# Variances with one token to a partition, inverses spread by TensorE into PSUM, and part of the pre-summing moved to DVE, in an adaLN block on Trainium2

## The reference, cut to what matters

```python
mod = (silu(c) @ wmod).reshape(2, 6, 1, -1)
sa, ca, ga, sb, cb, gb = mod[:, 0], ..., mod[:, 5]
ga, gb = (sign * max(|g|, 0.25) for g in (ga, gb))
h = layernorm(x) * (1 + ca) + sa
# per feature: a 2x2 softmax of inner products over the 2048 tokens mixes the two samples
x = x + ga * (h + msg(h))
h = layernorm(x) * (1 + cb) + sb
x = x + gb * ffn(h)       # down( silu(h Wgate) * (h Wup) ), width 2752
```

## Time and profile before

| what | value |
|---|---|
| median of 3 runs | 2818.89 us (2817.76 to 2823.97) |
| profiled execution, its own time | 2821.63 us |
| its span | 2819.8 us |
| mean granted TensorE clock, share of full | 0.992 |
| TensorE busy (matmul) | 2750.6 us, 98% |
| DVE busy | 1545.2 us, 55% |
| ACT busy | 1059.7 us, 38% |
| POOL busy | 156.1 us, 6% |

### The profile page before, as it was taken

The page is one execution under the profiler, slowest core; times in us unless marked ns, Lnnn a source line. Parts: engine busy times, 40 slices in busy tenths (PEclk is TensorE's granted clock), DMA queues, the critical chain, the costliest instruction groups (busy, mean ns, idle before and its releaser), DMA issues.

```text
span 2819.8 us, 32541 instructions
## 1 busy us (share of the span) xinstructions
PE 2750.6 (98%) x11784; PEld 2157.2 (77%) x11784; DVE 1545.2 (55%) x2057; ACT 1059.7 (38%) x1616; POOL 156.1 (6%) x206
## 2 busy tenths in 40 slices
PE   8988999998999999999999899999999999999999
PEld 3336887786888886788887788887788888888887
DVE  6988777764455534455443433335446446446544
ACT  4656455553243432334423211112343333333332
POOL 5200011000010000000100000000000000000000
PEclk9999999999999999999999999999999999999999
DMA  8675999989788879888879999999757657657654
GB/s 343 241 288 195 334 329 325 334 301 342 267 300 304 305 256 299 287 309 301 294 271 283 348 358 344 352 348 320 252 212 256 227 210 250 233 211 245 245 202 165
DMA packets 359711, 795.77 MB, mean 282 GB/s; under 512 B 25760, under 2 KB 154016, under 8 KB 350848
## 3 DMA queue, kind: packets, MB, share of 16 engines
q1 hardware_dynamic: 341648, 721.32, 73.3%
q0 software_dynamic: 17088, 59.78, 6.2%
q10 hardware_dynamic: 816, 12.58, 1.1%
HBM read 553.26 MB, written 240.32 MB: 281 GB/s over the span
## 4 chain that ended last, share of the span: by engine, by line
PE 86%; DMA 3%; issue 1%; SPq 1%; ACT 1%; DVE 1%; DVEq 0%; ACTq 0%
PE ps L1588 19%; PE ps L1589 19%; PE ps L1590 19%; PE ps L1651 10%; PE ps L1652 10%; PE ps L1653 10%; DMA x_raw_P<-xr_dram 1%; DMA h_dram<-ww 1%; DMA w_raw<-wdn 0%; SPq L397 0%; SPq L388 0%; DMA whl_dram<-w_lo_P 0%; PE ps L1598 0%; ACT x_raw_P L737 0%; PE ps L1599 0%
## 5 line engine op out<-in xcount | busy, mean ns | idle before, releaser
L1588 PE MATMUL ps<-x_hi_P,w_slot 128*128 128x512 f32 (+1 forms) x1848 | 724.5, 392 | 23.1 <-ACT vv L803 10.5
L1589 PE MATMUL ps<-x_lo_P,w_slot 128*128 128x512 f32 (+1 forms) x1848 | 723.2, 391 | 0.0
L1590 PE MATMUL ps<-x_hi_P,w_slot 128*128 128x512 f32 (+1 forms) x1848 | 722.9, 391 | 0.0
L1651 PE MATMUL ps<-hh,w_hi 128*128 128x512 f32 (+1 forms) x1232 | 481.1, 391 | 3.3 <-DVE w_lo L1354 2.0
L1652 PE MATMUL ps<-hl,w_hi 128*128 128x512 f32 (+1 forms) x1232 | 480.9, 390 | 0.0
L1653 PE MATMUL ps<-hh,w_lo 128*128 128x512 f32 (+1 forms) x1232 | 479.9, 389 | 0.0
L1588 PEld LDWEIGHTS ps<-x_hi_P,w_slot 128*128 128x128 f32 (+1 forms) x1848 | 344.4, 186 | 104.9 <-ACT vv L803 11.7
L1590 PEld LDWEIGHTS ps<-x_hi_P,w_slot 128*128 128x128 f32 (+1 forms) x1848 | 344.4, 186 | 78.3
L1589 PEld LDWEIGHTS ps<-x_lo_P,w_slot 128*128 128x128 f32 (+1 forms) x1848 | 344.5, 186 | 77.4
L1354 DVE TENSOR_TENSOR w_lo<-w_raw,w_hi 128x1408 fp32r<-128x1408 f32 x112 | 181.7, 1623 | 212.6 <-ACT w_hi L870 212.6
L1651 PEld LDWEIGHTS ps<-hh,w_hi 128*128 128x128 f32 (+1 forms) x1232 | 231.6, 188 | 53.3 <-DVE w_lo L1354 2.4
(11 more groups left out here) (181 smaller groups left out, 2651.6 us busy)
## 6 DMA issues: line engine op xcount, KB each, us to landing
w_slot<-whl_dram SPq DMA_DIRECT2D x420, 512.0 KB, 6.1
w_raw<-wds_dram SPq DMA_DIRECT2D x64, 704.0 KB, 4.6
hl_raw<-h_dram SPq DMA_DIRECT2D x56, 768.0 KB, 7.0
h_dram<-hb SPq DMA_DIRECT2D x30, 1280.0 KB, 9.8
whl_dram<-w_hi SPq DMA_DIRECT2D x140, 256.0 KB, 3.4
whl_dram<-w_lo_P SPq DMA_DIRECT2D x140, 256.0 KB, 4.2
w_raw<-wdn SPq DMA_DIRECT2D x48, 704.0 KB, 5.0
hl_raw<-h_dram SPq DMA_DIRECT2D x28, 1024.0 KB, 9.8
```

What stands on the lines that cost most here:

```text
L1588: mm(bank, hi[:, w], x_hi[name][:, k, :], start=fresh and k == 0, stop=False, skip_group_check=not fresh)
L1589: mm(bank, hi[:, w], x_lo[name][:, k, :], start=False, stop=False, skip_group_check=not fresh)
L1590: ins = mm(bank, lo[:, w], x_hi[name][:, k, :], start=False, stop=k == KH - 1, skip_group_check=not fresh)
L1651: mm(bank, hi[0:n, w], hh[stage % 2][0:n, j, :], start=fresh and j == 0, stop=False, skip_group_check=not fresh)
```

## The change

The variance is formed with tokens on the partitions: for each 128 tokens, TensorE takes 128 columns of `sq_pair` as weights and one column of ones as the moving side, so a chunk's variances are a 128x4 tile in PSUM. Root (ACT) and reciprocal (DVE) work on 128x4. ACT then makes four diagonal 128x128 matrices from the identity and these inverses (`diagonal`), and TensorE multiplies them by ones (`spread`), which puts the 512 inverses into every row of a PSUM bank; `normalise` reads that bank. For u = 1 the banks are the ones of `ps_mean[1]`, so the means of u = 1 of half 1 wait until half 0 is normalised. DVE adds tiles 0 to 3 of three of the four chunks of half 0, POOL of one. Stores of the normalised pairs are issued in halves of 2 MB. The order on TensorE is written anew.

```diff
+    eye_all = sb("eye_all", [P], F32, 184 * K)
+    std = sb("std", [2, 2, NTB], F32, 185 * K)
+    inv = sb("inv", [2, 2, NTB], F32, 185 * K + 64)
+    diag = sb("diag", [2, NTB, P], F32, 192 * K)
...
+    RSTD_BANK = (6, 2)
...
@@ POOL
                 if t == 0:
-                    sum_tiles(0, 0)
                     sum_tiles(0, 1)
-                    sum_tiles(1, 0)
-                    add_squares(0, 0)
-                    sum_tiles(1, 1)
-                else:
-                    add_squares(0, 0)
+                add_squares(0, 0)
                 add_squares(0, 1)
@@ ACT
+                def diagonal(u, h):
+                    i = t * 4 + 2 * u + h
+                    act.wait_ge(inv_ready, i + 1)
+                    if i >= 2:
+                        act.wait_ge(rstd_ready, i - 1)
+                    for b in range(NTB):
+                        ins = s.activation(diag[:, h, b, :], eye_all[:], ACT.Identity, scale=inv[:, u, h, b:b + 1])
+                    ins.then_inc(diag_ready, 1)
...
                 for u, h in ((0, 0), (0, 1), (1, 0), (1, 1)):
                     square(u, h, range(NSQ // 2))
                     if (u, h) != (0, 0):
                         root(u if h else 0, 1 - h)
                     square(u, h, range(NSQ // 2, NSQ))
+                    if (u, h) != (0, 0):
+                        diagonal(u if h else 0, 1 - h)
                 root(1, 1)
-                square_sums(0, range(KD))
-                save_xhat(0)
-                square_sums(1, range(KD // 2))
+                square_sums(0, range(KD // 2))
+                save_xhat(0, 0)
+                square_sums(0, range(KD // 2, KD - 1))
+                diagonal(1, 1)
+                square_sums(0, range(KD - 1, KD))
+                save_xhat(0, 1)
                 if t:
                     copy_rows(0)
+                square_sums(1, range(KD // 2))
+                if t == 0:
+                    save_xhat(1, 0)
+                square_sums(1, range(KD // 2, KD - 2))
+                if t:
                     copy_rows(1)
-                square_sums(1, range(KD // 2, KD))
+                square_sums(1, range(KD - 2, KD))
                 if t == 0:
-                    save_xhat(1)
+                    save_xhat(1, 1)
@@ DVE
                 def invert(u, h):
-                    v.reciprocal(rstd[:, u, h, :], std[:, h, :]).then_inc(rstd_ready, 1)
+                    v.reciprocal(inv[:, u, h, :], std[:, u, h, :]).then_inc(inv_ready, 1)
+                def sum_tiles(u, h):
...
+                    v.tensor_tensor(two, xk[:, 0:2, :], xk[:, 2:4, :], ALU.add).then_inc(presum_chain, 1)
+                    dve.wait_ge(presum_chain, summed[0])
+                    v.tensor_tensor(presums[u][:, h, :], two[:, 0, :], two[:, 1, :], ALU.add).then_inc(presum_dve, 1)
                 def normalise(u, k):
-                        v.scalar_tensor_tensor(dbuf[u][:, :, k, b, :], dbuf[u][:, :, k, b, :], 1.0,
-                                               rstd[:, u, :, b * CC:(b + 1) * CC], ALU.mult, ALU.mult,
+                        v.scalar_tensor_tensor(dbuf[u][:, :, k, b, :], ps[:, RSTD_BANK[u]:RSTD_BANK[u] + 2, b * CC:(b + 1) * CC], 1.0,
+                                               dbuf[u][:, :, k, b, :], ALU.mult, ALU.mult,
...
+                if t == 0:
+                    sum_tiles(0, 0)
                 centre(0, 0)
+                if t == 0:
+                    sum_tiles(1, 0)
                 centre(0, 1)
+                if t == 0:
+                    sum_tiles(1, 1)
                 centre(1, 0)
                 invert(0, 0)
                 centre(1, 1)
                 invert(0, 1)
...
                 for u in range(2):
-                    dve.wait_ge(rstd_ready, t * 4 + (2 * u + 4))
+                    dve.wait_ge(rstd_ready, t * 4 + (2 * u + 2))
                     for k in range(KD):
                         normalise(u, k)
...
-                        if u == 0 and k in (2, 4):
-                            invert(1, (k - 2) // 2)
+                        if u == 0 and k in (3, 5):
+                            invert(1, (k - 3) // 2)
@@ TensorE, means
-                    if t:
-                        pe.wait_ge(centred, 2 * (i + 1))
+                    if t and u == 0:
+                        pe.wait_ge(std_ready, i + 1)
+                    if t and u == 1:
+                        pe.wait_ge(xhat_ready, 4 * KD)
@@ TensorE, variances and spread
-                        mm(ps_var[h], ones[:], sq_pair[:, j % 2, :], start=j == 0, stop=j == NSQ - 1).then_inc(sq_pair_used, 1)
-                        if group is not None:
-                            modulate(group, part_of, range(2 * j, 2 * j + 2))
+                        for b in range(NTB):
+                            ins = mm(ps_mean[u][h][:, b:b + 1], sq_pair[:, j % 2, b * P:(b + 1) * P], ones[:, 0:1],
+                                     start=j == b == 0, stop=j == NSQ - 1 and b == NTB - 1)
+                        ins.then_inc(sq_pair_used, 1)
+                def spread(u, h):
+                    pe.wait_ge(diag_ready, t * 4 + (2 * u + h + 1))
+                    if t and u == 0:
+                        pe.wait_ge(xhat_ready, 2 * KD)
+                    mm(ps[:, RSTD_BANK[u] + h, :], ones[:], diag[:, h].rearrange("p b q -> p (b q)"), start=True, stop=True).then_inc(
+                        rstd_ready, 1)
@@ TensorE, order
+                means(0, 0)
+                means(0, 1)
                 if t == 0:
-                    means(0, 0)
-                    means(0, 1)
                     means(1, 0)
                     variances(0, 0)
                     means(1, 1)
                     variances(0, 1)
+                    spread(0, 0)
+                    variances(1, 0)
+                    spread(0, 1)
                     pe.wait_ge(silu_ready, 1)
-                    parts(0, range(2))
-                    variances(1, 0, 0, 2)
-                    variances(1, 1, 0, 3)
+                    parts(0, range(1))
+                    variances(1, 1)
+                    spread(1, 0)
+                    parts(0, range(1, 2))
+                    spread(1, 1)
+                    parts(0, range(2, 3))
                 else:
-                    means(0, 0)
-                    means(0, 1)
+                    parts(0, range(3, GROUP[0]))
                     means(1, 0)
                     means(1, 1)
-                    variances(0, 0, 0, 4)
-                    variances(0, 1, 0, 5)
-                    variances(1, 0, 1, 0)
-                    variances(1, 1, 1, 1)
-                    parts(1, range(2, GROUP[1]))
-            pe.wait_ge(eye_loaded, 16)
-            pe.wait_ge(centred, 16)
-            parts(2, range(4))
+                    variances(0, 0)
+                    variances(0, 1)
+                    parts(1, range(1))
+                    spread(0, 0)
+                    spread(0, 1)
+                    variances(1, 0)
+                    parts(1, range(1, 2))
+                    spread(1, 0)
+                    variances(1, 1)
+                    parts(1, range(2, 3))
+                    spread(1, 1)
+                    parts(1, range(3, GROUP[1]))
+            pe.wait_ge(eye_loaded, 32)
             turn(0, ps_mod[0], ROWS[0] + ROWS[1], 0)
             turn(1, ps_mod[0], ROWS[0] + ROWS[1], ROWS[0])
-            parts(2, range(4, GROUP[2]))
+            parts(2, range(GROUP[2]))
```

More of the change, by code:

```diff
@@ L48 @@
 PRE = (4, 0)
+NTB = T // P
 assert NPAIR == 4 and sum(GROUP) == NPART and 2 * WPART == BLOCK and GROUP[0] == GROUP[1] == 2 * WM_RING
@@ L294, in bc, with tok2 @@
         return ap[:, None, :].broadcast_to([P, n, T])
+    def tok2(ap):
+        return ap.rearrange("p h k b c -> p h k (b c)")
     def tok(ap):
@@ L552, in sum_tiles @@
                 def sum_tiles(u, h):
-                    i = 2 * u + h
-                    pool.wait_ge(x_loaded[u][h], t * 16 + 16)
-                    pool.wait_ge(mean_mm, t * 4 + (i + 1))
+                    pool.wait_ge(x_loaded[u][h], 16)
                     xk, to = tok(xbuf[u][:, h]), presums[u][:, h, :]
-                    for k in range(1, PRE[t]):
+                    for k in range(1, PRE[0]):
                         ins = g.tensor_tensor(to, xk[:, 0, :] if k == 1 else to, xk[:, k, :], ALU.add)
-                        if k < PRE[t] - 1:
+                        if k < PRE[0] - 1:
                             ins.then_inc(pool_chain, 1)
@@ L644, in _, with save_xhat @@
             for t in range(NPAIR // 2):
[L645 to L650, removed]
+                def save_xhat(u, half):
+                    act.wait_ge(xhat_ready, t * (4 * KD) + 2 * KD * u + KD * (half + 1))
+                    first, ks = 4 * t + 2 * u + 2, slice(half * KD // 2, (half + 1) * KD // 2)
+                    s.dma_start(xhat_dram[first:first + 2].rearrange("h p (k w) -> p h k w", k=KD)[:, :, ks],
+                                tok2(dbuf[u][:, :, ks])).then_inc(xh_stored[u], 16)
```

(32 more changed lines are left out.)

40 lines of the change are left out of this document (22 added, 18 removed).

## The result

The changed kernel takes 2851.79 us (median of 4 runs, 2849.61 to 2852.64) against 2821.43 (median of 4, 2817.76 to 2824.74) of the kernel before in the same comparison: 1.011 times as long, 95% interval 1.0095 to 1.0126, or 30.4 us more. The profiled execution took 2851.85 us with a span of 2850.1, 30.3 more than before. The forecast was 21.6 more, 2840.5, in the range 2826 to 2853: the result lies inside it, 1.2 us from its upper end and 11.3 from the forecast's own number.

A forecast was written before the change was run, and what follows sets the result against it. DVE was taken to set most of the first phase, TensorE's written order its last 8 us. The turn's +7.6 and +14.0 for four more parts behind it sum to +21.6 on 2818.9: 2840.5 us, range 2826 to 2853.

The forecast's parts named there:

- DVE's gain: First phase: eight reciprocals of 3.35 us become 128x4 ones taken at 0.2, a gain of 25.2 us on DVE.
- Step 1: Start to half 0's normalising: centrings, pre-sums and reciprocals, then a diagonal and a spread; N = 43.3 us (41.4 to 45.2).
- cold term: Bound for TensorE's granted clock before the turn's end: -1.9 to +7 us.
- variance records far from 0.12: Sign of a wrong forecast: TensorE's records in the new variance matmuls were priced at 0.12 us each.
- bounds for the clock and for the records: TensorE: clock -1.9 to +7 us; records of the new variances up to +9, not together with the clock.
- TensorE cold through the variances of half 1: Rival: one-column matmuls and waits leave half 1's parts and spreads at clock 0.50, 10 us more: +32, 2851; chance 0.14.
- the two pre-sums on DVE: Half 0, before normalising: two added pre-sums cost DVE 3.8 us, with two of their four adds hit by POOL.
- Step 2: Half 0, from the start of normalising to its last spread, `spread(1,1)`: 22.4 us, with DVE stalling 5.2.
- Step 3: From half 0's last spread to half 1's normalising: 60.1 us, its core DVE's 13 us stall for mean (1,0).
- Step 4: Last normalising, in half 1: it ends at 42.6 us and the turn at 42.9, counted from its start.
- Step 5: Behind the turn: eight parts instead of four stand before `mean_f(0)`, +14.0 us, with DVE waiting 17.
- One for one: Network behind the first product: a shift of that product moves the end equally, since the network has no slack.

The follow-up runs named there:

- Run 1: Changed kernel with the variance matmuls moving all 128 columns of the ones in place of one column: 2839.15 us, ratio 1.0066.
- run 4: Changed kernel with the pre-sums of (1,0) and (1,1) in half 0 back on POOL, DVE keeping only (0,0): 2850.12 us, ratio 1.0112.
- run 3: Changed kernel with ACT making each half's last diagonal behind the row-summed squares of one tile instead of seven: 2842.94 us, ratio 1.0084.
- run 2: Changed kernel with parts 3 to 5 of group 0 in half 1 behind the means of u = 1: 2848.38 us, ratio 1.0105.
- run 5: Changed kernel with parts 0 to 3 of group 2 back ahead of the turn of groups 0 and 1: 2849.48 us, ratio 1.0102.
- run 7: Changed kernel with the 128-column variance matmuls and the early last diagonal together: 2830.12 us, ratio 1.0036.
- run 6: Changed kernel with each of the eight spreads done twice: 2856.39 us, ratio 1.0131.
- Run 8: On top of run 7, half 1 reordered: parts 3 to 5 where TensorE waited, group 1 behind the last spread, its ACT copies later: 2825.21 us, ratio 1.0018.
- run 9: Kernel before the change, with half 1's 4 MB store of pair (0) issued after the softmax exponential: 2810.91 us, ratio 0.9974.

## Why the prediction was right, and where its size was off

- **DVE's gain goes nowhere.** Right. Its idle time behind the spreads alone is 28.9 us, more than the 25.2 of the reciprocals.
- **Step 1, the start of half 0's normalising: the step that failed.** 51.77 instead of 43.3, +8.5. The step summed DVE's work, one diagonal and one spread, and put TensorE's work in between at nothing. But `spread(0,1)` is written behind the variances of (1,0). The diagonal was done at 45.07, 2.8 us behind the forecast's 42.3; the spread began at 49.60, when the 32 records were through, and took 2.05. The sum priced such records at 0.12 us, the full-clock pitch; at the half clock they cost 0.21, the means of (1,1) 5.90 us instead of 3.60, and the first spreads 1.93 and 2.05 instead of 1.0. Run 1 gives 6.5 of the 8.5 us back; the order on TensorE remains, for there too the spread waits for the variances, 1.4 us (the diagonal is done at 41.68, the spread starts at 43.10).
- **The range held by its cold term.** One of the forecast's own signs of being wrong came up, variance records far from 0.12, and the first product came at 264.6 and not near 252. Without its bounds for the clock and for the records the range would have ended at 21.6 + 4.2 + 2.1 + 1.9, or +30 on 2818.9, under the measured time. What happened is nearer to the forecast's own rival, "TensorE cold through the variances of half 1", at +10 and a chance of 0.14. Its total, 2851, fits by luck: it looked for the loss in half 1 alone and at 10 us, while run 1 shows 11.2, of which 6.5 stood before half 0's normalising. The Trainium skill (TensorE: Matmul & The Clock Gate, Part 1) has it that the array's default state is throttled and that activity releases it. The trace agrees with the direction that the rival took from this: 0.50 from 43.0 to 49.7 us. The records covered 6.70 of 6.70 us there.
- **Step 1, the two pre-sums on DVE.** The sum took clashes in two of their four adds; all four were slower (1.47 and 1.64 us, then 1.38 and 1.64, in the timeline, against 1.23 and 0.69 alone). That is 2.3 us against the 2.1 of the sum, but no cost (run 4): their cover is TensorE's lateness.
- **Step 2.** 51.77 to 74.30 is 22.5; forecast 22.4. ACT's order before the last diagonal is a cost of its own, some 9 us over both halves (run 3), which the forecast had inside its steps 2 and 4.
- **Step 3.** 74.30 to 136.77 is 62.5; forecast 60.1. The wait of 13 us before the third centring was 12.05. Its reading as the core was wrong: run 2 removes it and gains nothing. The sum up to the spreads, by which the step was worked out, was right.
- **Step 4.** 42.0 to the end of the turn, forecast 42.9.
- **Step 5.** The centring begins 34.9 us after the turn instead of 21.1: +13.8, forecast +14.0. But it is no separate loss: moving four parts ahead of the turn moves the turn (run 5).
- **Behind it** the forecast let everything move as one. 2.6 us were added (the second eight records of the second layernorm's variances, at 223.6 us, took 6.40 us instead of 3.70), and the stretch behind the first product was 3.9 shorter, within its own scatter. "One for one" holds no closer than that.

Against 21.6: +8.5 in step 1, +2.4 in step 3, -0.9 in step 4, -0.2 in step 5, +2.6 behind it, -3.9 in the network, +0.3 from step 2 and rounding, make 30.4. Theory of the whole: TensorE's chain. Of the 34.5 us by which the first product is later, counted from the first centring, the half clock and the waits for ACT's diagonal are 23.7 together (run 7), and the spreads some 6 (run 6), a part of that again at half clock. The rest, some 5 us, was not taken apart. Run 8 brings the new scheme to within 6.4 us of the old one by the median and 9.8 by the first product, of which 4.6 are its waits for loads.

## What to carry to other kernels

When an engine is full in the shares, ask whether another one's written order runs unbroken through the same stretch: freeing the first then only turns its work into waiting. To tell a wait that costs from one that only shows, move the work in front of it: if the wait turns up again further on and the end stays, the chain is elsewhere. Read the granted clock of the stretches with new small matmuls, also where the engine shows no gap: here matmuls with one moving column were cheap by their records, and the clock fell to half in and behind them; with 128 columns the records cost nearly the same and the clock stayed full up to the next long wait. And count the places of a timeline from a common event, since executions do not begin alike.

## What the runs showed of the hardware that was not expected

TensorE's granted clock was 0.50 while its records covered 6.70 of 6.70 us of one-column matmuls; with 128 columns and nothing else changed it stayed at 1.00 through the same matmuls (run 1). Sixteen records of the wide form took 1.95 us against 1.84, both at full clock, so the wide form costs next to nothing. And a 4 MB store on ACT's queue held back 1 MB loads on SP's: the slowest of eleven took 13.5 us to land beside it, at most 6.4 with the store moved (run 9), the median one 4.9 and 4.8, and moving it was worth 7.6 us to the kernel before.
